# Last layer's edges of a four-layer graph network: messages built in place in PSUM, and the scan of maxima reads them there

## The chip, the cores and the metric

One program on one core of a Trainium2 chip. The metric is the device time of one execution in microseconds (us), the median of the runs shown. The engines are TensorE (PE, its weight loads PEld), VectorE (DVE), ScalarE (ACT), GpSimd (POOL) and SyncE (SP).

## The reference, cut to what matters

Four graph layers run over 3125 nodes of 128 features and 100000 edges, sorted by their target node; each layer is followed by a residual and a layer norm. Only the edges of the last layer are touched. The target's part of a message doesn't vary within a segment, so the kernel adds it after the maximum; what the edge stage computes is, for each edge, the source's row plus weight times `ww`, and of these the running maximum over each segment of equal targets:

```python
Wd, Ws, ww = (Wm[:H], Wm[H:2 * H], Wm[2 * H])
msgs = z[edge_dst] @ Wd + z[edge_src] @ Ws + edge_weight[:, None] * ww[None, :] + bm
agg = jax.ops.segment_max(msgs, edge_dst, num_segments=n)
```

## The kernel before

The edges are laid on 128 partitions (lanes) of T = 784 edges each (the last lane is padded). `layer3_edges` goes through them in TURNS = 28 turns of BODY = 28 edges for each lane, a turn in two halves of HALF = 14. `m.table3` in HBM holds the product of each node's row with `Ws` (the source part); `m.rows3` in HBM takes the running maxima, one row for each edge, and `layer3_nodes` later picks the last row of every segment.

What each engine does in a turn, in the order of its own queue, is written out by hand; only semaphores tie the queues together:

- POOL (lines 2350 to 2362) gathers the source rows: one indirect DMA for each edge position, 128 rows of 512 bytes, into `feat[h]`. Half 0 takes 14 of them, half 1 takes HALF - FOUND = 10 (in turn 0 both take 14). Before a half's gathers it waits for the indices (`staged`) and for `summed`, which says that the half's earlier content of `feat[h]` has been added.
- PE (2436 to 2446) finds the other FOUND = 4 rows of half 1: 75 matmuls of three bf16 parts of the table with one-hot matrices `hot[b]` (25 blocks) into bank 0 of PSUM (`found`), and after ScalarE has copied that out (2423), 4 transposes into bank 2 (`rows_found`). The one-hots of a turn are made by VectorE in the turn before: the first 13 around the scan of half 0, the other 12 around the scan of half 1 (one ahead of the scan, the rest behind it). PE's loop (2438) asks for them 7 blocks ahead.
- ACT: `scale` (2382) writes for each edge position `edge_w` times that edge's weight, 14 or 10 activations of 128 elements, into `scaled_w`, which lies in banks 4 to 7 of PSUM, edge by edge, features contiguous. `turn_back` (2401) reorders the maxima of the half before into `rows[h]` for the store; `spread_resets` (2395) writes the resets of a coming half; `next_indices` (2377) stages the indices of the next turn's gathers. Their order in the loop is: scale of half 0, turn_back of half 1 of the turn before, spread_resets of half 1, the copy of `found`, next_indices of half 0, scale of half 1, turn_back of half 0, spread_resets of the next half 0, next_indices of half 1.
- DVE, `half` (2474): a copy (2477) carries the last maxima of the half before into column 0 of `msg`; the add (2481) writes `feat + scaled_w` into `msg`, which is laid out feature by feature with 15 positions each (so the add's output steps 15 elements); in half 1 four operations (2487) make the messages of the found rows; then the scan (2497) goes over all 128 x 15 = 1920 positions: `state = max(state + resets, msg)`, written to `maxima[h]`. `resets[h]`, `msg` and `maxima[h]` all lie in SBUF (the arena).
- SP loads the keys of the one-hots (2324) and stores `rows[h]` (2328), 896 KB for each half.

There is one `msg` and one `scaled_w`; `feat`, `maxima`, `resets` and `rows` have two buffers each.

Of the kernel before, what the change touches and what calls it, by code (L numbers as in the profile page):

```python
# [9 lines left out]
ALU = mybir.AluOpType  # L10
ACT = mybir.ActivationFunctionType
# [3 lines left out]
N, D, E = 3125, 128, 100000  # L15
# [3 lines left out]
HALF = 14  # L19
# [24 lines left out]
FOUND = 4  # L44
# [12 lines left out]
BIG = 1e30  # L57
# [2221 lines left out]
def layer3_edges(nc, m, I):  # L2279

    with phase(nc, "layer3_edges") as sem:
        A = Arena(m)
        feat = [A(HALF, D) for _ in range(2)]
        msg = A(D, HALF + 1)
        maxima = [A(D, HALF + 1) for _ in range(2)]
        rows = [A(HALF, D) for _ in range(2)]
        tab = A(NB, D)
# [5 lines left out]
        act_vals = A(BODY)  # L2293
        idx = [A(HALF, dt=I32) for _ in range(2)]
        block_ids = A(NB)
        ps = m.psum
        found = ps[:, 0, :]
        rows_found = ps[:, 2, :].rearrange("p (k f) -> p k f", f=D)
        scaled_w = ps[:, 4:8, :].rearrange("p a (k f) -> p (a k) f", f=D)[:, 0:HALF, :]

        begun = sem("states_begun")
        ids_made = sem("block_ids_made")
# [6 lines left out]
        summed, found_summed, carried, scanned = sem("messages_summed"), sem("found_messages_summed"), sem("maxima_carried"), sem("halves_scanned")  # L2309
# [6 lines left out]
        with nc.Block() as block:  # L2316
# [47 lines left out]
            @block.scalar  # L2364
            def _(eng):
                for h in range(2):
                    eng.activation(idx[h], m.src[:, h * HALF:(h + 1) * HALF], ACT.Copy).then_inc(staged[h], 1)

                def split():
                    for k, (a, b) in enumerate(TAB_HALF):  # L2370
                        eng.wait_ge(tab_in[k], 16)
                        eng.activation(parts[0][:, a:b, :], tab[:, a:b, :], ACT.Copy).then_inc(high_made, 1)
                    for k, (a, b) in enumerate(TAB_HALF):
                        eng.wait_ge(rest_made, k + 1)
                        eng.activation(parts[1][:, a:b, :], tab[:, a:b, :], ACT.Copy).then_inc(mid_made, 1)

                def next_indices(i, h, before):

                    hold(eng, landed[h], 16 * before)
                    eng.activation(idx[h], m.src[:, bass.ds(i * BODY + BODY + h * HALF, HALF)], ACT.Copy).then_inc(staged[h], 1)  # L2380

                def scale(i, h, n):

                    eng.wait_ge(summed, 2 * i + h + 1)
                    if h == 0:
                        if not isinstance(i, int):
                            eng.wait_ge(found_summed, i * FOUND - FOUND + 1)
                        eng.activation(act_vals, m.val[:, bass.ds(i * BODY, BODY)], ACT.Copy).then_inc(vals_staged, 1)
                        eng.wait_ge(vals_staged, i + 1)
                    for j in range(n):  # L2390
                        s = h * HALF + j
                        t = eng.activation(scaled_w[:, j, :], m.edge_w[:, :], ACT.Copy, scale=act_vals[:, s:s + 1])
                    t.then_inc(scaled, 1)

                def spread_resets(i, h):

                    hold(eng, scanned, 2 * i + h)
                    eng.activation(resets[h][:, :, 1:HALF + 1],
                                   spread(m.reset[:, bass.ds(i * BODY + h * HALF, HALF)], 1, [P, D, HALF]), ACT.Copy).then_inc(spread_out[h], 1)

                def turn_back(i, h):

                    eng.wait_ge(scanned, 2 * i + h + 2)
                    eng.wait_ge(stored[h], 16 * i + 16)
                    eng.activation(rows[h], maxima[h][:, :, 1:HALF + 1].rearrange("p f t -> p t f"), ACT.Copy).then_inc(turned_back[h], 1)

                eng.wait_ge(begun, 2)
                spread_resets(0, 0)
                spread_resets(0, 1)
                scale(0, 0, HALF)  # L2410
                split()
                next_indices(0, 0, HALF)
                scale(0, 1, HALF)
                turn_back(0, 0)
                spread_resets(1, 0)
                next_indices(0, 1, HALF)
                with eng.Fori(1, TURNS) as i:
                    scale(i, 0, HALF)
                    turn_back(i - 1, 1)
                    spread_resets(i, 1)  # L2420
                    eng.wait_ge(hot_used, i * NB + NB)
                    eng.wait_ge(turned, i)
                    eng.activation(turned_rows, found, ACT.Copy).then_inc(evicted, 1)
                    next_indices(i, 0, i * HALF + HALF)
                    scale(i, 1, HALF - FOUND)
                    turn_back(i, 0)
                    spread_resets(i + 1, 0)
                    next_indices(i, 1, i * (HALF - FOUND) + HALF)
                turn_back(TURNS - 1, 1)
# [19 lines left out]
            def _(eng):  # L2449
# [24 lines left out]
                def half(i, h, n, before, hots):  # L2474

                    eng.wait_ge(scanned, 2 * i + h + 1)
                    eng.tensor_copy(msg[:, :, 0], maxima[1 - h][:, :, HALF]).then_inc(carried, 1)
                    eng.wait_ge(landed[h], 16 * before)
                    eng.wait_ge(scaled, 2 * i + h + 1)
                    by_edge = msg.rearrange("p f t -> p t f")  # L2480
                    eng.tensor_tensor(by_edge[:, 1:n + 1, :], feat[h][:, 0:n, :], scaled_w[:, 0:n, :], ALU.add).then_inc(summed, 1)  # L2481
                    if n < HALF:
                        eng.wait_ge(turned, i + 1)
                        eng.wait_ge(vals_staged, i + 1)
                        for j in range(n, HALF):
                            s = h * HALF + j
                            eng.scalar_tensor_tensor(out=by_edge[:, j + 1, :], in0=m.edge_w[:, :], scalar=act_vals[:, s:s + 1],  # L2487
                                                     in1=rows_found[:, j - n, :], op0=ALU.mult, op1=ALU.add).then_inc(found_summed, 1)
                    for hot_of in hots[:1]:
                        one_hot(*hot_of)  # L2490
                    eng.wait_ge(spread_out[h], i + 1)
                    eng.wait_ge(carried, 2 * i + h + 1)
                    eng.wait_ge(summed, 2 * i + h + 2)
                    if n < HALF:
                        eng.wait_ge(found_summed, i * FOUND + 1)
                    eng.wait_ge(turned_back[h], i)
                    eng.tensor_tensor_scan(maxima[h].rearrange("p f t -> p (f t)"), resets[h].rearrange("p f t -> p (f t)"),  # L2497
                                           msg.rearrange("p f t -> p (f t)"), -BIG, ALU.add, ALU.max).then_inc(scanned, 1)
                    for hot_of in hots[1:]:
                        one_hot(*hot_of)  # L2500

# [225 lines left out]
```

## Time and profile before

| | us |
|---|---|
| median of 3 runs | 5445.45 (5445.11 to 5450.29) |
| profiled execution, its own time | 5450.11 |
| span of the profiled execution | 5448.4 |
| PE, DVE, ACT, POOL busy | 1991.3 (37%), 3728.0 (68%), 2105.0 (39%), 3924.3 (72%) |
| last layer's edges: first gather to last scan's end | 4329.3 to 5369.7 |

The page of the profile sums over eleven stages that run one behind the other with a barrier between them, so busy shares of the whole span say little about this one. The stage of the change is 1040 us long, from 4329 to 5370 us of the span, and its turns repeat closely; one turn from the middle, from 4800 to 4836 us, is shown for each engine. In a timeline row stand the start, the duration, the engine, the line, the operation with output<-input, how many alike are merged, and in brackets how long the engine sat idle before it and what ended that.

### The profile page before, as it was taken

To read this page: it belongs to the slowest core of one execution; us is meant where nothing else is said; L and a number is where in the kernel's file an instruction comes from. 1 tells how busy PE (TensorE), PEld (TensorE's weight loads), DVE (VectorE), ACT (ScalarE), POOL (GpSimd) and SP (SyncE) were. 2 spreads that over 40 slices of the span, in tenths; PEclk is the share of its full clock that TensorE was granted. 3 is DMA by queue.
4 is the path that set the end of the run, shared out by engine and by line. 5 is a ranking of instruction groups with operands and counts; after the bars stand their busy time and mean duration, and the time that the engine had idled before them with its cause. 6 is when DMAs were issued, how large, how long until landed. Compare 5 with 4: busy or idle time off the path is not lost. (4 is left out here: it accounts for less than half of the span.)

```text
span 5448.4 us, 55911 instructions
## 1 busy us (share of the span) xinstructions
PE 1991.3 (37%) x9749; PEld 999.4 (18%) x9749; DVE 3728.0 (68%) x7733; ACT 2105.0 (39%) x5941; POOL 3924.3 (72%) x2991
## 2 busy tenths in 40 slices
PE   2699999999500000000011000000000556665664
PEld 1354444444300000000011000000000322222222
DVE  9676666665578888888876666666666665656665
ACT  0333333332328778778731000000000354454442
POOL 0688888887168777777725888888886188878774
PEclk9899999999755555555555555555555777777777
DMA  9555555555336666666643555555554123232232
GB/s 403 158 103 102 97 98 95 99 102 108 85 102 243 222 236 227 246 236 230 223 169 131 173 174 176 171 168 171 176 175 139 36 93 101 93 102 92 94 102 67
DMA packets 283514, 819.47 MB, mean 150 GB/s; under 512 B 63269, under 2 KB 178485, under 8 KB 271250
## 3 DMA queue, kind: packets, MB, share of 16 engines
q1 hardware_dynamic: 99250, 504.98, 25.1%
q0 software_dynamic: 171504, 252.10, 21.3%
q10 hardware_dynamic: 12528, 60.37, 2.7%
q14 instruction: 219, 1.79, 0.1%
q8 instruction: 13, 0.21, 0.0%
HBM read 368.73 MB, written 448.51 MB: 150 GB/s over the span
## 5 line engine op out<-in xcount | busy, mean ns | idle before, releaser
L1864 POOL DMA_INDIRECT arena<-table,arena x784 | 989.5, 1262 | 238.9 <-issue 238.9
L624 POOL DMA_INDIRECT tab<-arena x560 | 986.9, 1762 | 189.7 <-issue 147.3
L2353 POOL DMA_INDIRECT arena<-table,arena x676 | 824.1, 1219 | 206.6 <-issue 205.5
L746 PE MATMUL psum<-arena 128*128 128x512 bf16 (+1 forms) x4704 | 958.9, 359 | 0.0
L1514 PE MATMUL psum<-ident,arena 128*128 128x128 f32 x15 | 3.7, 428 | 2533.9 <-DVEq L1542 2533.9
L1287 POOL DMA_INDIRECT arena<-table,arena x588 | 719.8, 1224 | 189.4 <-issue 178.1
L2440 PE MATMUL psum<-arena 128*128 128x512 bf16 x2025 | 580.1, 455 | 290.6 <-DVE arena L2472 171.0
L1333 ACT ACTIVATE arena<-arena 128x128 f32<-128x128 f32 x1974 | 598.7, 387 | 186.1 <-DVE arena L1441 123.6
L1441 DVE SCALAR_TENSOR_TENSOR arena<-arena 128x512 f32<-128x512 f32 x728 | 544.9, 749 | 13.4 <-issue 1.2
L746 PEld LDWEIGHTS psum<-arena 128*128 128x128 bf16 x4704 | 436.4, 99 | 480.6 <-issue 36.7
L1514 PEld LDWEIGHTS psum<-ident,arena 128*128 128x128 f32 x15 | 2.7, 213 | 2534.6 <-DVEq L1542 2534.4
L2481 DVE TENSOR_TENSOR arena<-arena,psum 128x1792 f32<-128x1792 f32 (+1 forms) x56 | 155.6, 2779 | 402.4 <-DMA arena<-table,arena 326.9
L781 ACT ACTIVATE arena<-psum 128x387 f32<-128x387 f32 x224 | 99.0, 442 | 695.2 <-POOLq L623 509.7
L1935 DVE TENSOR_TENSOR arena<-arena 128x1792 f32<-128x1792 f32 x56 | 113.5, 2027 | 352.5 <-DMA arena<-table,arena 245.4
L2440 PEld LDWEIGHTS psum<-arena 128*128 128x128 bf16 x2025 | 221.7, 113 | 645.1 <-issue 258.7
L682 DVE SCALAR_TENSOR_TENSOR arena<-arena 128x128 f32<-128x128 f32 x784 | 277.0, 353 | 25.4 <-issue 3.2
L1963 DVE SCALAR_TENSOR_TENSOR arena<-arena 128x136 f32<-128x136 f32 x784 | 274.4, 350 | 16.7 <-DVE arena L1956 15.9
L1926 DVE SCALAR_TENSOR_TENSOR arena<-arena 128x128 f32<-128x128 f32 x784 | 269.9, 344 | 15.9 <-issue 8.8
L649 DVE SCALAR_TENSOR_TENSOR arena<-arena 128x3 f32<-128x3 f32 x224 | 49.6, 221 | 322.1 <-ACT arena L781 321.9
L1287 POOL DMA_INDIRECT xT<-table,arena x196 | 223.2, 1139 | 59.8 <-issue 58.8
L671 DVE TENSOR_SCALAR arena<-arena 128x3125 bf16<-128x3125 f16 x224 | 237.8, 1062 | 0.9 <-PE psum L746 0.9
L2497 DVE TENSOR_TENSOR_SCAN arena<-arena 128x1920 f32<-128x1920 f32 x56 | 232.3, 4148 | 0.4 <-DVE arena L2487 0.2
(408 smaller groups left out, 4595.2 us busy)
## 6 DMA issues: line engine op xcount, KB each, us to landing
rows<-arena SPq DMA_DIRECT2D x56, 3808.0 KB
arena<-seg_rows SPq DMA_DIRECT2D x112, 896.0 KB
rows<-arena SPq DMA_DIRECT2D x56, 1008.0 KB
seg_rows<-arena ACTq DMA_DIRECT2D x28, 1792.0 KB
rows<-arena SPq DMA_DIRECT2D x56, 896.0 KB
arena<-table,arena POOLq DMA_INDIRECT x2048
arena<-src_lanes SPq DMA_DIRECT2D x56, 448.0 KB
tab<-arena POOLq DMA_INDIRECT x560
```

What stands on the lines that cost most here:

```text
L624: eng.indirect_dma_start(out=m.tabs[j], out_offset=bass.IndirectOffsetOnAxis(ap=idx[g][:, k:k + 1], axis=0), in_=rows[g][:, k, 0:D], in_of ...
L671: eng.tensor_scalar(hot[n % HOTS], m.node_ids, of[:, CENTRED, s:s + 1], None, ALU.is_equal).then_inc(hot_made, 1)
L682: eng.scalar_tensor_tensor(out=xr[h][:, j, :], in0=prev, scalar=keeps[:, s:s + 1], in1=xr[h][:, j, :], op0=ALU.mult, op1=ALU.add).then_inc ...
L746: t = eng.matmul(ps[:, c, 0:w], part[n // 2 % PAIRS][:, n % 2, :], hot[n % HOTS][:, lo:lo + w], start=False, stop=False, skip_group_check= ...
L1287: eng.indirect_dma_start(out=feat[k][:, j, :], out_offset=None, in_=m.table1, in_offset=bass.IndirectOffsetOnAxis(ap=idx[k][:, j:j + 1], a ...
L1333: eng.activation(apart[:, t, r * D:(r + 1) * D], feat[k][:, t, 0:D], ACT.Copy, scale=hot[k % 2][:, t, r:r + 1]).then_inc(masked, 1)
L1441: v.put(eng.scalar_tensor_tensor(out=row[:, j, 0:SUM], in0=row[:, j - 1, 0:SUM] if j else old, scalar=keeps[h][:, j:j + 1], in1=apart[:, j ...
L1864: eng.indirect_dma_start(out=kv[k][:, j, :], out_offset=None, in_=m.table2, in_offset=bass.IndirectOffsetOnAxis(ap=idx[k][:, j:j + 1], axi ...
L1926: eng.scalar_tensor_tensor(out=q[k][:, j, :], in0=q[k][:, j - 1, :] if j else q[k - 1][:, HALF - 1, :], scalar=carry_keeps[k % 2][:, j:j + ...
L1963: v.put(eng.scalar_tensor_tensor(out=row[:, j, 0:MAX], in0=row[:, j - 1, 0:MAX] if j else old, scalar=keeps[h][:, j:j + 1], in1=row[:, j, ...
L2353: eng.indirect_dma_start(out=feat[h][:, j, :], out_offset=None, in_=m.table3, in_offset=bass.IndirectOffsetOnAxis(ap=idx[h][:, j:j + 1], a ...
L2440: t = eng.matmul(found, part[:, b, :], hot[b], start=(b == 0 and p == 0), stop=(b == NB - 1 and p == 2))
```

## The change

`msg` moves from SBUF to banks 4 to 7 of PSUM, over the place of `scaled_w`, which is gone. ScalarE writes the scaled weights straight into the places of the messages (steps of 15 elements), VectorE adds the gathered rows to them in place, and the scan reads its second input from PSUM; `resets` and `maxima` stay in SBUF. Since the one buffer is now written by `scale`, `scale` of a half waits until the scan of the half before has read it (`scanned` in place of `summed`), and the wait for `found_summed` ahead of it goes. The carry copy moves from ahead of the add, before the wait for the gathered rows, to behind it.

```diff
-        msg = A(D, HALF + 1)
...
-        scaled_w = ps[:, 4:8, :].rearrange("p a (k f) -> p (a k) f", f=D)[:, 0:HALF, :]
+        msg = ps[:, 4:8, :].rearrange("p a c -> p (a c)")[:, 0:D * (HALF + 1)]
+        by_edge = msg.rearrange("p (f t) -> p t f", t=HALF + 1)
...
                 def scale(i, h, n):
 
-                    eng.wait_ge(summed, 2 * i + h + 1)
+                    eng.wait_ge(scanned, 2 * i + h + 1)
                     if h == 0:
-                        if not isinstance(i, int):
-                            eng.wait_ge(found_summed, i * FOUND - FOUND + 1)
                         eng.activation(act_vals, m.val[:, bass.ds(i * BODY, BODY)], ACT.Copy).then_inc(vals_staged, 1)
                         eng.wait_ge(vals_staged, i + 1)
                     for j in range(n):
                         s = h * HALF + j
-                        t = eng.activation(scaled_w[:, j, :], m.edge_w[:, :], ACT.Copy, scale=act_vals[:, s:s + 1])
+                        t = eng.activation(by_edge[:, j + 1, :], m.edge_w[:, :], ACT.Copy, scale=act_vals[:, s:s + 1])
                     t.then_inc(scaled, 1)
...
                     eng.wait_ge(scanned, 2 * i + h + 1)
-                    eng.tensor_copy(msg[:, :, 0], maxima[1 - h][:, :, HALF]).then_inc(carried, 1)
                     eng.wait_ge(landed[h], 16 * before)
                     eng.wait_ge(scaled, 2 * i + h + 1)
-                    by_edge = msg.rearrange("p f t -> p t f")
-                    eng.tensor_tensor(by_edge[:, 1:n + 1, :], feat[h][:, 0:n, :], scaled_w[:, 0:n, :], ALU.add).then_inc(summed, 1)
+                    eng.tensor_tensor(by_edge[:, 1:n + 1, :], feat[h][:, 0:n, :], by_edge[:, 1:n + 1, :], ALU.add).then_inc(summed, 1)
+                    eng.tensor_copy(by_edge[:, 0, :], maxima[1 - h][:, :, HALF]).then_inc(carried, 1)
...
                     eng.tensor_tensor_scan(maxima[h].rearrange("p f t -> p (f t)"), resets[h].rearrange("p f t -> p (f t)"),
-                                           msg.rearrange("p f t -> p (f t)"), -BIG, ALU.add, ALU.max).then_inc(scanned, 1)
+                                           msg, -BIG, ALU.add, ALU.max).then_inc(scanned, 1)
```

## Rows read from the trace of the kernel before

**Rows 1.** Waits of VectorE and GpSimd, 4400 to 5360 us: who, for whom, total, times, longest.

```profile
DVE arena L2481 <- DMA arena<-table,arena: 289.5, 40, 8.9
...
POOL arena L2353 <- issue: 191.8, 629, 0.3
POOL arena L2353 <- DVE arena L2481: 0.3, 1, 0.3
```

**Rows 2.** Gathers grouped: whole run, then the first 18, then one turn, 4800 to 4836.44.

```profile
L2353 POOL DMA_INDIRECT arena<-table,arena x676 | 824.1, 1219 | 206.6 <-issue 205.5 <-ACT arena L2367 0.8 <-DVE arena L2481 0.3
...
L2353 POOL DMA_INDIRECT arena<-table,arena x18 | 17.1, 947 | 6.0 <-issue 5.2 <-ACT arena L2367 0.8
...
L2353 POOL DMA_INDIRECT arena<-table,arena x25 | 33.8, 1351 | 7.6 <-issue 7.3 <-DVE arena L2481 0.3
```

**Rows 3.** Timeline of GpSimd, one turn from held gather to held gather.

```profile
4798.74 4.63 POOL L2353 DMA_INDIRECT arena<-table,arena  x1 [0.30 <-issue]
...
4816.17 0.94 POOL L2353 DMA_INDIRECT arena<-table,arena  x1 [0.30 <-issue]
4817.42 3.70 POOL L2353 DMA_INDIRECT arena<-table,arena  x1 [0.31 <-issue]
...
4832.67 0.95 POOL L2353 DMA_INDIRECT arena<-table,arena  x1 [0.31 <-issue]
...
4835.18 4.64 POOL L2353 DMA_INDIRECT arena<-table,arena  x1 [0.30 <-DVE arena L2481]
```

**Rows 4.** Timeline of VectorE in that turn.

```profile
4798.47 4.14 DVE L2497 TENSOR_TENSOR_SCAN arena<-arena 128x1920 f32<-128x1920 f32 x1
...
4812.77 2.32 DVE L2481 TENSOR_TENSOR arena<-arena,psum 128x1280 f32<-128x1280 f32 x1 [6.28 <-DMA arena<-table,arena]
4814.93 1.18 DVE L2487 SCALAR_TENSOR_TENSOR arena<-edge_w,arena,psum 128x128 f32<-128x128 f32 x4
4815.96 0.34 DVE L2472 TENSOR_SCALAR arena<-arena 128x512 bf16<-128x512 f16 x1
4816.21 4.16 DVE L2497 TENSOR_TENSOR_SCAN arena<-arena 128x1920 f32<-128x1920 f32 x1
4820.28 3.45 DVE L2472 TENSOR_SCALAR arena<-arena 128x512 bf16<-128x512 f16 x11
4823.66 0.26 DVE L2477 COPY arena<-arena 128x128 f32<-128x128 f32 x1
4831.61 3.21 DVE L2481 TENSOR_TENSOR arena<-arena,psum 128x1792 f32<-128x1792 f32 x1 [7.69 <-DMA arena<-table,arena]
...
4834.91 4.16 DVE L2497 TENSOR_TENSOR_SCAN arena<-arena 128x1920 f32<-128x1920 f32 x1
```

**Rows 5.** Timeline of VectorE and GpSimd behind the stage: a scan with a PSUM input.

```profile
5378.19 0.42 DVE L2633 TENSOR_TENSOR_SCAN arena<-whole_neg,psum 128x128 f32<-128x128 f32 x1 [0.39 <-PE psum L2596]
5378.34 0.95 POOL L2548 DMA_INDIRECT arena<-rows,first_end  x1 [19.12 <-POOLq L103]
```

**Rows 6.** Timeline of ScalarE in that turn.

```profile
4816.50 4.16 ACT L2392 ACTIVATE psum<-edge_w,arena 128x128 f32<-128x128 f32 x14
4820.60 3.28 ACT L2405 ACTIVATE arena<-arena 128x1792 f32<-128x1792 f32 x1
4823.78 1.69 ACT L2398 ACTIVATE arena<-reset 128x1792 f32 x1
4837.81 0.60 ACT L2423 ACTIVATE arena<-psum 128x512 f32<-128x512 f32 x1 [12.34 <-DMA arena<-table]
4838.41 2.98 ACT L2392 ACTIVATE psum<-edge_w,arena 128x128 f32<-128x128 f32 x10
```

**Rows 7.** Timeline of TensorE, then its busy time and granted clock, 4820.6 to 4835.

```profile
4820.66 13.25 PE L2440 MATMUL psum<-arena 128*128 128x512 bf16 x51 [2.85 <-DVE arena L2472]
...
4820.60:4835.00 14.40, 13.25 (x51) 5.41 (x51) 0.85 0.38 123
```

**Rows 8.** An add in layer 2 with contiguous operands, grouped, 2946 to 4157 us.

```profile
L1935 DVE TENSOR_TENSOR arena<-arena 128x1792 f32<-128x1792 f32 x56 | 113.5, 2027 | 352.5 <-DMA arena<-table,arena 245.4 <-issue 107.1
```

## The prediction

> **What bounds the kernel now.** I read the waits of the stage first, because eleven stages run one behind the other and the page's busy shares mix them. VectorE waits 289.5 us for gathered rows ahead of its add, while GpSimd, which issues the gathers, waits for an engine once, for 0.3 us; all its other idle time is "issue", 0.3 us ahead of each gather [rows 1]. So the gathers set the length of the turns, and VectorE, ScalarE and TensorE follow.
>
> Then I asked what a gather costs. The first 18 of the stage, before any scan, take 947 ns each; over all 676 the mean is 1219, in the sample turn 1351 [rows 2]. The timelines say which are long: the gather issued at 4798.74 takes 4.63 us, the one at 4817.42 takes 3.70, the one at 4835.18 takes 4.64 [rows 3]. Put beside VectorE [rows 4]: scans run from 4798.47 to 4802.61, from 4816.21 to 4820.37 and from 4834.91 to 4839.07, and the three long gathers end 0.76, 0.75 and 0.75 us behind those ends. The gather at 4816.17, issued 0.04 us ahead of a scan, takes 0.94. A gather issued while the scan runs is held until it ends. Gathers issued within the add (4832.67, inside 4831.61 to 4834.82) take 0.95. The add has one input in SBUF and one in PSUM; the scan has both in SBUF.
>
> A turn is 4835.18 - 4798.74 = 36.44 us: 24 gathers at 1.25 us (0.947 and 0.30 of issue), 30.0, and two holds, 3.68 and 2.75 us, together 6.4.
>
> **The holds.** The change leaves the scan one SBUF input, the resets. What the trace shows of such operations is that gathers pass beside them at full speed: the add above, and, nearer, the only scan of the run with a PSUM input, 5378.19 to 5378.61: a gather issued at 5378.34 within it takes 0.95 us, where a hold until 0.75 us behind its end would have made it 1.02 [rows 5]. I take the holds as gone; the other end is that none goes. Their sum: 676 x (1.219 - 0.947) = 184 us [rows 2]; about 2 us of it I leave standing, by estimate, for the two subtractions of `split`, which keep two SBUF inputs. Gain 182 us. By the sample turn it is 27 x 6.4 + 3.7 = 177.
>
> The Trainium skill (SBUF — State Buffer, Who interferes with whom) says that a VectorE instruction with two SBUF inputs takes the read interface it shares with GpSimd and shuts out a GpSimd instruction that reads SBUF. By that rule the holds go, and the rows agree for the scans. The same place infers that `tensor_tensor` leaves descriptor generation alone, since that would need the write interface; taken so, the scan wouldn't hold either, and the gain would be nil; the 4.63 us gathers speak against it.
>
> **The scan itself.** 1920 elements take 4.16 us from SBUF, the 128 of the PSUM scan 0.42 [rows 4, 5]: a slope of (4.16 - 0.42) / 1792 = 2.09 ns an element, and 1920 x 2.09 = 4.01 leaves 0.15 fixed, 0.27 + 0.15 = 0.42 for 128. Both lie on one line, so reading PSUM costs the scan nothing.
>
> **Steps of 15 elements in PSUM.** No row shows them; bounds from both sides. ScalarE's scale is 4.16 us for 14, 0.297 each [rows 6]. It moves from contiguous to stepped writes. Lower bound: no change. Upper: what a stepped access costs ScalarE in SBUF, 3.28 us for 1792 elements against 1.69 [rows 6], 0.89 ns an element, 0.11 us an operation: +1.6 us for 14, +1.1 for 10. The add (3.21 and 2.32 us [rows 4]) writes in steps already, into SBUF; with contiguous operands 1792 elements take 2.03 [rows 8]. Lower bound: PSUM takes steps at no cost, 2.03, so -1.2 us. Upper: its read is stepped now as well and costs as much as ScalarE's, +1.6 and +1.1. I take both as unchanged, since the add's own row with a stepped write is nearest; the upper end decides a rival. The Trainium skill (Advanced Engine Details and Errata, PSUM Cachelines) has lines of 8 bytes there and asks for pairs of consecutive elements; steps of 60 bytes never give one. By that the upper end would be the likelier.
>
> **The waits.** One buffer now serves `scale`, add and scan, so two loops get tighter, and 30.0 us is the turn they must fit in.
> Loop A, scan to scale to add to scan, over both halves: scale 4.16 + 0.23 for staging the weights + 2.98, adds 3.21 + 2.32, found rows 1.18, copies 2 x 0.26, one-hots ahead of the scans 2 x 0.34, scans 2 x 4.16 [rows 4, 6], with six handovers of 0.1: 24.2 us. It has 5.8 us to spare; at the upper bounds (+5.4) it is 29.6.
> Loop B goes through TensorE: one-hots are made behind the scan of half 1, 51 matmuls follow, `found` is copied out, and only then does ScalarE's queue reach the scale of half 1. From the scan's end at 4820.37 to the copy at 4837.81 is 17.4 us, the copy and the scale of 10 are 3.6 [rows 6], and from the add of half 1 to the scan's end VectorE takes 7.6, plus the copy that is now there, 0.26 [rows 4]: 28.9 us. Before, this scale was followed by 7.8 us of waiting for rows (4841.4 to 4849.2), so it cost nothing. Now 1.1 us are left. With the upper bounds, +2.2, it is 31.1.
>
> What else is queued: behind the longer wait of `scale` on ScalarE stand turn_back, which waits for the same scan anyway, spread_resets and next_indices. For half 0 they are due only when the copy of `found` comes, 12 us later [rows 6]. The indices of the next half 0 stand behind the copy of `found`, 0.2 us later; by loop B's times they come some 2 us before GpSimd is through with the ten gathers of half 1. SP's stores depend on turn_back and stay two buffers ahead. The carry copy was hidden in the wait for rows and comes to stand on VectorE's path, 0.26 us a half; while the gathers bound the turn it costs only at the last half, 0.3 us. The wait for `found_summed` was past whenever the scan is. The new end of each path is the landing of the gathers again, in turns of 30.0 us.
>
> **Sum.** Profiled execution 5450.1 - 182 + 0.3 = 5268. The median of the runs is 4.7 us under it: 5264.
>
> **Rivals.**
> 1. A loop takes over. Stepped PSUM accesses cost the upper bounds, or TensorE's clock is low in the 51 matmuls (it is 0.85 of full speed there, between its two levels, and 13.25 us busy [rows 7]; at 1.2 GHz, half, they would be 22.5). For: loop B has 1.1 us of room. Against: TensorE stood idle for 2.85 us ahead of this stretch [rows 7], and shorter turns leave less idle time. Upper bounds: (31.1 - 30.0) x 27 = 30 us back, 5294; twice these: 33.3, 5353; the low clock alone, (28.9 + 22.5 - 13.25 - 30.0) = 8.2 at worst, 5485 at the far end; as the clock was low for part already, I price it at half, 4.6 us a turn, which gives 33.5 and 5359.
> 2. The hold belongs to the scan as such, not to its second SBUF input. The turn stays 36.4 us; time 5445. For: every hold of the stage proper is a scan's. Against: the scan of [rows 5], a margin of 0.07 us.
> 3. Slower: stepped writes and in-place adds in PSUM are several times dearer. It decides once loop B grows by 7.5 us, past 36.4. With 5 ns an element: ten scales 10 x (0.64 + 0.19 - 0.30) = +5.3, the add 1280 x 5 ns + 0.1 - 2.32 = +4.2, the found rows 4 x 0.5 = +2: 40.4 us a turn, 27 x 4.0 more than now, 5553. Nothing in the trace is that dear (the worst step here is 1.8 ns an element).
>
> **How the numbers follow.** Forecast 0.70 (5264), rival 1 0.19, rival 2 0.07, rival 3 0.04. Range: the forecast with some 10 us for the holds' sum, and rival 1 up to a turn of 32.6 us (2.6 x 27 = 70), 5255 to 5335. A measurement can tell 0.2% (11 us) from no change. Faster: forecast and nearly all of rival 1, 0.89; same: rival 2, 0.07; slower: rival 3, 0.04.
>
> **What would show it.** Right: gathers of 947 ns mean throughout with none over 1.1 us beside a scan, a turn of 30.0 us, and VectorE still waiting for rows ahead of its add. Rival 1: GpSimd waits for ScalarE's indices or VectorE's add, the add waits for `scale`. Rival 2: gathers of 4.6 us remain. The operations at 2392 and 2481 show the price of the steps at once. The prediction fails most easily in loop B, by 1.1 us of room in a turn.

## The result

The changed kernel took 5274.39 us (median of 4 runs, 5271.81 to 5275.44) against 5447.78 us before, measured beside it: ratio 0.9681, 95% interval 0.9664 to 0.9698, 173 us faster. 5264 was forecast, in a range of 5255 to 5335. Run again later on two other chips (below), the same file gave this time on one and 5520 us, slower than before, on the other, so part of this document is about why the forecast held and part about why it doesn't hold everywhere.

The profiled execution took 5273.86 us, with a span of 5272.1. First the grouped lines of the changed kernel over the stage: busy time, mean ns of one, then idle time ahead.

```profile
L2353 POOL DMA_INDIRECT arena<-table,arena x676 | 671.9, 994 | 208.2 <-issue 203.4 <-DVE psum L2477 3.4 <-ACT arena L2367 0.8
...
L2494 DVE TENSOR_TENSOR_SCAN arena<-arena,psum 128x1920 f32<-128x1920 f32 x56 | 232.4, 4150 | 0.5 <-DVE psum L2484 0.2
...
L2390 ACT ACTIVATE psum<-edge_w,arena 128x128 f32<-128x128 f32 x676 | 201.5, 352 | 143.6 <-DVE arena L2494 142.7
...
L2477 DVE TENSOR_TENSOR psum<-arena,psum 128x1792 f32<-128x1792 f32 x29 | 58.8, 2029 | 268.5 <-DMA arena<-table,arena 268.5
L2477 DVE TENSOR_TENSOR psum<-arena,psum 128x1280 f32<-128x1280 f32 x27 | 40.4, 1497 | 42.6 <-DMA arena<-table,arena 42.6
L2484 DVE SCALAR_TENSOR_TENSOR psum<-edge_w,arena,psum 128x128 f32<-128x128 f32 x108 | 30.3, 349 | 0.0
```

The gathers answer [rows 2]: 824.1 us have become 671.9, the mean 1219 ns has become 994. The scan is as long as it was [rows 4]. The in-place add takes 2029 ns where it took 3.21 us [rows 4], as much as the contiguous add of [rows 8]. The scale keeps its length. Then the timeline of one turn, VectorE's rows first, GpSimd's behind them.

```profile
4936.64 4.15 DVE L2494 TENSOR_TENSOR_SCAN arena<-arena,psum 128x1920 f32<-128x1920 f32 x1
4940.71 3.83 DVE L2470 TENSOR_SCALAR arena<-arena 128x512 bf16<-128x512 f16 x12
4946.05 1.50 DVE L2477 TENSOR_TENSOR psum<-arena,psum 128x1280 f32<-128x1280 f32 x1 [1.52 <-DMA arena<-table,arena]
...
4949.04 4.15 DVE L2494 TENSOR_TENSOR_SCAN arena<-arena,psum 128x1920 f32<-128x1920 f32 x1
4953.10 2.96 DVE L2470 TENSOR_SCALAR arena<-arena 128x512 bf16<-128x512 f16 x11
4965.74 2.03 DVE L2477 TENSOR_TENSOR psum<-arena,psum 128x1792 f32<-128x1792 f32 x1 [9.68 <-DMA arena<-table,arena]
...
4940.98 0.94 POOL L2353 DMA_INDIRECT arena<-table,arena  x1 [0.30 <-issue]
...
4950.97 0.94 POOL L2353 DMA_INDIRECT arena<-table,arena  x1 [0.30 <-issue]
4952.22 0.94 POOL L2353 DMA_INDIRECT arena<-table,arena  x1 [0.30 <-issue]
4953.47 2.71 POOL L2353 DMA_INDIRECT arena<-table,arena  x1 [0.31 <-issue]
4956.48 0.94 POOL L2353 DMA_INDIRECT arena<-table,arena  x1 [0.30 <-issue]
```

Gathers now pass within the scan of 4949.04 to 4953.19 at 0.94 us, and none of the 165 that the stage issues within a scan takes more than 0.95; the holds of [rows 3] are gone. But one gather is still long, and it is a new kind: issued at 4953.47, 0.37 us into the row of 11 one-hots that follows the scan of half 1, it ends at 4956.18, 0.12 behind the end of that row (4956.06). The row of 12 at 4940.71 holds nobody; its operations are 0.32 us apart (3.83 / 12) where those of the closed row are 0.27 apart (2.96 / 11). 17 of the 27 turns have such a gather, 2.62 to 2.79 us long, and take about 31.8 us; most of the others take 30.0. That is some 17 x 1.75 = 30 us that the prediction has no word for.

Last, the waits over 4400 to 5200 us (who, for whom, total, times, longest), beside [rows 1].

```profile
DVE psum L2477 <- DMA arena<-table,arena: 285.1, 52, 9.8
...
ACT psum L2390 <- DVE arena L2494: 136.3, 26, 6.4
...
ACT arena L2421 <- PE psum L2438: 97.0, 26, 4.9
...
POOL arena L2353 <- DVE psum L2477: 2.4, 8, 0.3
```

VectorE still waits for rows and GpSimd for almost nobody: the gathers still set the turn. ScalarE, which before sat idle for under 1 us in all directly ahead of its scales, now waits 136.3 us there for the scan of half 0, and it costs nothing: the add behind it still waits for rows.

Where the 176.25 us between the two profiled executions (5450.11 and 5273.86) lie, by the first and last gather of the stage: the gather stretch went from 1029.9 to 879.3 us (150.6), it begins 16.2 us earlier (4313.1, not 4329.3), and what lies behind its end shrank from 89.2 to 79.7 us (9.5). But for 1.6 us between the last gather and the last scan, the last two terms are in code that the change doesn't touch.

### The profile page after: what moved, and what is told of

It is laid out like the page before. It is cut to its first block and busy times, and to the rows that moved or that the text cites. A ratio compares the mean times of both kernels' runs of the same rounds, so it can differ in the third digit from the quotient of the medians.

```text
span 5272.1 us, 55718 instructions
## 1 busy us (share of the span) xinstructions
PE 1925.0 (37%) x9583; PEld 990.1 (19%) x9749; DVE 3665.7 (70%) x7733; ACT 2103.1 (40%) x5941; POOL 3773.8 (72%) x2991
## 3 DMA queue, kind: packets, MB, share of 16 engines
q1 hardware_dynamic: 99250, 504.98, 26.3%
## 5 line engine op out<-in xcount | busy, mean ns | idle before, releaser
L1864 POOL DMA_INDIRECT arena<-table,arena x784 | 995.6, 1270 | 238.8 <-issue 238.8
L746 PE MATMUL psum<-arena 128*128 128x512 bf16 (+1 forms) x4592 | 930.1, 358 | 6.3 <-issue 0.4
L1287 POOL DMA_INDIRECT arena<-table,arena x588 | 710.7, 1209 | 183.9 <-issue 178.3
L2353 POOL DMA_INDIRECT arena<-table,arena x676 | 671.9, 994 | 208.2 <-issue 203.4
L2438 PE MATMUL psum<-arena 128*128 128x512 bf16 x1971 | 530.6, 434 | 306.1 <-DVE arena L2470 263.3
L2477 DVE TENSOR_TENSOR psum<-arena,psum 128x1792 f32<-128x1792 f32 (+1 forms) x56 | 99.3, 1772 | 311.1 <-DMA arena<-table,arena 311.1
L2390 ACT ACTIVATE psum<-edge_w,arena 128x128 f32<-128x128 f32 x676 | 201.5, 352 | 143.6 <-DVE arena L2494 142.7
L1884 ACT ACTIVATE arena<-src 128x14 int32 x56 | 12.0, 214 | 566.4 <-DMA arena<-table,arena 566.2
```

Of the source, the lines that this page charges most:

```text
L746: t = eng.matmul(ps[:, c, 0:w], part[n // 2 % PAIRS][:, n % 2, :], hot[n % HOTS][:, lo:lo + w], start=False, stop=False, skip_group_check= ...
L1287: eng.indirect_dma_start(out=feat[k][:, j, :], out_offset=None, in_=m.table1, in_offset=bass.IndirectOffsetOnAxis(ap=idx[k][:, j:j + 1], a ...
L1864: eng.indirect_dma_start(out=kv[k][:, j, :], out_offset=None, in_=m.table2, in_offset=bass.IndirectOffsetOnAxis(ap=idx[k][:, j:j + 1], axi ...
L2353: eng.indirect_dma_start(out=feat[h][:, j, :], out_offset=None, in_=m.table3, in_offset=bass.IndirectOffsetOnAxis(ap=idx[h][:, j:j + 1], a ...
L2390: t = eng.activation(by_edge[:, j + 1, :], m.edge_w[:, :], ACT.Copy, scale=act_vals[:, s:s + 1])
L2438: t = eng.matmul(found, part[:, b, :], hot[b], start=(b == 0 and p == 0), stop=(b == NB - 1 and p == 2))
```

## The experiments

Twelve runs in four jobs, each job on one chip with the kernel before timed beside it. The table shows all of them, by what their profiles say of the stage: the stretch from first to last gather, the mean gather, and how long behind the end of the scan of half 1 the copy of `found` starts (us, range over the turns without the first of them).

| kernel | chip | us | ratio to before, interval | stretch | gather ns | copy of `found` |
|---|---|---|---|---|---|---|
| before | - | 5445.45 | | 1029.9 | 1219 | 17.3-18.9 |
| after | - | 5274.39 | 0.9681 [0.9664, 0.9698] | 879.3 | 994 | 11.5-14.2 |
| e4 before again | 14 | 5443.99 | one run | 1029.3 | 1218 | 17.5-19.0 |
| e1 waits alone | 14 | 5445.28 | 0.9997 [0.9987, 1.0006] | 1031.6 | 1222 | 19.1-24.1 |
| e2 weights in SBUF | 14 | 5441.40 | 0.9998 [0.9989, 1.0008] | 1026.1 | 1030 | 25.0-26.0 |
| e3 row broken | 14 | 5519.56 | 1.0130 [1.0109, 1.0151] | 1094.5 | 951 | 26.4-30.6 |
| e5 turn back first | 10 | 5237.26 | 0.9625 [0.9609, 0.9641] | 846.6 | 948 | 12.9-14.5 |
| e6 after again | 10 | 5270.04 | 0.9684 [0.9668, 0.9700] | 871.7 | 983 | 11.5-14.3 |
| e7 = e2 | 4 | 5446.56 | 0.9990 [0.9978, 1.0001] | 1023.1 | 1029 | 25.1-25.9 |
| e8 = e3 | 4 | 5521.10 | 1.0131 [1.0102, 1.0161] | 1091.0 | 948 | 26.3-30.1 |
| e9 = after | 4 | 5520.03 | 1.0129 [1.0100, 1.0159] | 1090.6 | 951 | 26.9-30.1 |
| e10 = e5 | 9 | 5246.96 | 0.9634 [0.9606, 0.9662] | 846.5 | 948 | 12.8-14.5 |
| e11 copy of `found` last | 9 | 5252.93 | 0.9645 [0.9617, 0.9673] | 852.5 | 953 | 21.5-22.2 |
| e12 two parts | 9 | 5249.87 | 0.9639 [0.9609, 0.9670] | 860.0 | 966 | 9.3-10.7 |

The kernel before took 5443.54, 5440.37, 5449.13 and 5447.22 us (medians) on chips 14, 10, 4 and 9.

### The first job: what holds a gather

**e1**, the kernel before with the waits and the order of the changed one, the messages still in SBUF:

```diff
-                    eng.wait_ge(summed, 2 * i + h + 1)
+                    eng.wait_ge(scanned, 2 * i + h + 1)
                     if h == 0:
-                        if not isinstance(i, int):
-                            eng.wait_ge(found_summed, i * FOUND - FOUND + 1)
...
-                    eng.tensor_copy(msg[:, :, 0], maxima[1 - h][:, :, HALF]).then_inc(carried, 1)
...
+                    eng.tensor_copy(msg[:, :, 0], maxima[1 - h][:, :, HALF]).then_inc(carried, 1)
```

> The kernel before with only the new waits and order: scale waits for the scan of the half before, the carry copy stands behind the add; messages stay in SBUF. My theory: a gather issued while the scan reads two SBUF inputs is held, and nothing else of the change matters; the scans still hold gathers, so 5448 us within 0.2%, mean gather about 1219 ns. Rival, the new waits by themselves shift the turn enough to change the time: a turn more than 0.5 us off 36.4, over 13 us in all.

Measured: no difference, and gathers of 1222 ns as before. The waits by themselves give and cost nothing while the scans hold the gathers, though the copy of `found` comes later (19.1 to 24.1 us, where e4 has 17.5 to 19.0); the gain is in where the messages lie.

**e2**, the changed kernel with the scaled weights in SBUF, so that the add reads two SBUF operands and the scan one:

```diff
+        scaled_w = A(HALF, D)
...
-                        t = eng.activation(by_edge[:, j + 1, :], m.edge_w[:, :], ACT.Copy, scale=act_vals[:, s:s + 1])
+                        t = eng.activation(scaled_w[:, j, :], m.edge_w[:, :], ACT.Copy, scale=act_vals[:, s:s + 1])
...
-                    eng.tensor_tensor(by_edge[:, 1:n + 1, :], feat[h][:, 0:n, :], by_edge[:, 1:n + 1, :], ALU.add).then_inc(summed, 1)
+                    eng.tensor_tensor(by_edge[:, 1:n + 1, :], feat[h][:, 0:n, :], scaled_w[:, 0:n, :], ALU.add).then_inc(summed, 1)
```

> The changed kernel, but ScalarE writes the scaled weights contiguously to SBUF, so that the add has two SBUF inputs and one output in PSUM; the scan still reads PSUM. Theory (two SBUF inputs of VectorE hold the gathers): the scans hold none, the adds hold one gather each, for 0.2 to 1.8 us, about 1.9 us a turn, so some 50 us above the changed kernel's 5274: 5325. Rival (the hold belongs to the scan as an operation, and a plain add takes no part): 5274, no long gather beside an add.

The timeline of e2, one turn, VectorE and then GpSimd:

```profile
4716.98 2.03 DVE L2478 TENSOR_TENSOR psum<-arena 128x1792 f32<-128x1792 f32 x1 [8.66 <-DMA arena<-table,arena]
...
4719.56 4.15 DVE L2495 TENSOR_TENSOR_SCAN arena<-arena,psum 128x1920 f32<-128x1920 f32 x1
...
4734.60 1.50 DVE L2478 TENSOR_TENSOR psum<-arena 128x1280 f32<-128x1280 f32 x1 [7.18 <-ACT arena L2391]
...
4717.98 1.84 POOL L2354 DMA_INDIRECT arena<-table,arena  x1 [0.30 <-issue]
...
4720.13 0.94 POOL L2354 DMA_INDIRECT arena<-table,arena  x1 [0.30 <-issue]
...
4732.33 0.94 POOL L2354 DMA_INDIRECT arena<-table,arena  x1 [5.03 <-ACT arena L2381]
...
4734.83 2.08 POOL L2354 DMA_INDIRECT arena<-table,arena  x1 [0.30 <-issue]
```

The holds have moved from the scan to the add. A gather issued within the add of 4716.98 to 4719.01 takes 1.84 us and ends 0.81 behind it; the next, within the scan, takes 0.94. So a hold goes with VectorE reading two operands from SBUF, in the add as in the scan, and rival 2 (the scan as such) falls. The Trainium skill says the same of the read interface (SBUF — State Buffer, Who interferes with whom), and infers there that descriptor generation is left alone; these rows speak against the inference.

The trace of before could have settled rival 2 without a run. The subtractions of `split` read two SBUF operands and are no scans; VectorE's rows of them, and the gathers beside them:

```profile
4359.29 3.60 DVE L2463 TENSOR_TENSOR arena<-arena 128x1536 f32<-128x1536 f32 x2
4362.81 3.62 DVE L2466 TENSOR_TENSOR arena<-arena 128x1536 bf16<-128x1536 f32 x2
...
4360.55 1.36 POOL L2353 DMA_INDIRECT arena<-table,arena  x1 [0.31 <-issue]
4362.21 1.49 POOL L2353 DMA_INDIRECT arena<-table,arena  x1 [0.30 <-issue]
4364.01 1.37 POOL L2353 DMA_INDIRECT arena<-table,arena  x1 [0.30 <-issue]
4365.68 1.57 POOL L2353 DMA_INDIRECT arena<-table,arena  x1 [0.30 <-issue]
```

Each of the four holds one gather, until 0.82 us behind its own end. The size of e2's holds was as expected too: 676 x (1.030 - 0.947) = 56 us.

The time was not. 5325 was expected, 5441 came: GpSimd waits 5.03 us for ScalarE's indices (L2381), which stand behind the copy of `found`, and that comes 25 to 26 us behind the scan. Loop B of the prediction (through TensorE) had taken over.

**e3**, the changed kernel with a nop after every third one-hot, to open the closed row:

```diff
-                    for hot_of in hots[1:]:
+                    for k, hot_of in enumerate(hots[1:]):
                         one_hot(*hot_of)
+                        if k % 3 == 2:
+                            eng.engine_nop()
```

> The changed kernel with an empty operation on VectorE after every third one-hot behind the scan. In the changed kernel 17 gathers of 2.6 to 2.8 us end 0.1 us behind a row of eleven one-hots. Theory: back-to-back one-hots keep GpSimd out, and a gap lets the gather in; then nearly all of these are at most 1.1 us, 17 x 1.75 = 30 us less, 5245. Rival (the gap is too short, or the row holds as a whole, whatever stands in it): the long gathers stay, 5274 or a little more.

There was no held gather beyond the four of `split` and three of 1.1 us (mean 951), yet the time is 5519.56, 275 us above the 5245 expected. Read alone this says that breaking the row frees the gathers and that seven nops a turn cost 250 us; e8 and e9 show that neither follows.

**e4** is the kernel before, unedited, for its profile on that chip.

> The kernel before, unchanged, for a second profile. Between the first two profiles stages that the change doesn't touch differ by 16 us ahead of the last layer's edges and by 8 us behind them. If that comes with the program, this profile has the stage lengths of the first (layer 1 edges 1257 us, the last layer's nodes 71 us) within 2 us; if it is spread between executions, it does not.

It repeats the profile of before to 0.6 us in the stretch of gathers. Of the two stages that its expectation names, the last layer's nodes repeat (70.9 us against 70.7) and layer 1's edges don't (1252 against 1257): that much lies between two executions of one kernel.

### The second job: the held gather in the row of one-hots

**e5** has ScalarE turn the maxima back ahead of the scale of half 1, which moves the row of one-hots against the gathers:

```diff
                     next_indices(i, 0, i * HALF + HALF)
-                    scale(i, 1, HALF - FOUND)
                     turn_back(i, 0)
+                    scale(i, 1, HALF - FOUND)
```

> The changed kernel with ScalarE's turn_back of half 0 ahead of the scale of half 1, instead of behind it: no more work, 3.3 us more between that scan and the scaled weights. Loop B then is longer by 3.3 us. If gathers bound the turn with the room that the changed kernel's profile shows (copy of found 13.2 us behind the scan, loop B 24.7), nothing changes: 5274. If TensorE is as late as in the kernel before (17.4, loop B 28.9), the turn is 32.2 us and the time some 57 us over the changed kernel's.

**e6** is the changed kernel, unedited, on the same chip.

> The changed kernel, unchanged, a second time. In the profiles of the kernels with the waits alone, with the weights in SBUF and with the broken row, TensorE's marks come late: the copy of found starts 17 to 30 us behind the scan of half 1, against 11.5 to 14 in the changed kernel's first profile, and these profiles hold a third as many records of semaphore updates. If TensorE's lateness belongs to those programs, this run repeats the first: 5274 us, copy of found 11.5 to 14 us behind the scan, turns of 30.0 or 31.8. If it belongs to the chip or the recording, TensorE is late here too and loop B sets the turn: 33 to 37 us, 5350 to 5450.

e6 repeats the result. e5 is 33 us faster by the medians. Its grouped gathers and its row of one-hots:

```profile
L2353 POOL DMA_INDIRECT arena<-table,arena x676 | 640.9, 948 | 206.5 <-issue 196.6
...
4953.51 4.14 DVE L2494 TENSOR_TENSOR_SCAN arena<-arena,psum 128x1920 f32<-128x1920 f32 x1
4957.57 3.46 DVE L2470 TENSOR_SCALAR arena<-arena 128x512 bf16<-128x512 f16 x11
```

The row is 0.31 us an operation (3.46 / 11) and holds nobody; every turn takes 29.95 to 30.07 us. The stretch is 846.6 against 871.7: 25.1 us for the 13 held gathers of e6, 13 x 1.75 = 23, and two turns with an extra idle stretch of about 1 us. The other 8 us of the medians lie outside the stretch or between executions.

The edit shifted the phase, and the kept traces say which phase holds. All 37 gathers held by a row (17 in the changed kernel, 13 in e6, 1 in e11, 6 in e12) were issued 0.28 to 0.45 us behind the start of a row of 11. Between 0.34 and 0.45 us others pass, at 0.94 to 1.08; every one issued later passes. In e5 and e10 none falls into that stretch. Beside the rows of 12 none is held, though in the changed kernel and in e6 many are issued there too. Why the one row holds and the other doesn't is open. The Trainium skill (SBUF — State Buffer, Who interferes with whom) has `tensor_scalar` among the operations that can take both shared interfaces, for the whole instruction and for whoever issues first. One instruction is 0.27 us here, so a gather shut out for a row of 11 goes beyond what that says, and the rows beside which gathers pass show that it isn't the rule for every such row.

### The third job: the same program, 250 us apart

e1 to e4 had run on one chip and e5 and e6 on another, and in the first group TensorE was late throughout. So e2, e3 and the changed kernel went to one chip together.

> The kernel with the weights in SBUF (e2) once more, now on one chip with the kernel of the change and with the broken row. It took 5441 us and its copy of `found` came 25 to 26 us behind the scan of half 1, against 11.5 to 14 in the kernel of the change, but the two had been run in different jobs. If TensorE's lateness belongs to the program: 5441 again, stage 1049, copy of `found` 25 us behind the scan. If it belongs to the chip or the job: the copy comes some 12 to 14 us behind the scan in all three kernels of this job (or 20 or more in all three), and this one takes 5274 + 55 - 30 = about 5300, the holds beside the adds alone.

> The kernel with a nop after every third one-hot (e3) once more, on one chip with the kernel of the change. Program: 5520 again, GpSimd waiting some 250 us for ScalarE's indices, copy of `found` 27 to 30 us behind the scan. Chip or job: 5237 to 5245, no held gathers, the copy 12 to 14 us behind the scan.

> The kernel of the change, unedited, on the chip of the two before. Program: 5270 to 5274, stage 890 to 897, copy of `found` 11.5 to 14.5 us behind the scan of half 1, some 14 to 18 held gathers. Chip or job: a copy that comes over 20 us behind the scan, and a time over 5400.

e9 is the changed kernel, unedited, and takes 5520.03 us, 1.3% over the kernel before on the same chip (5449.13). The lateness goes with the chip or the job, not with the program; each job ran on a chip of its own, so the two can't be told apart. I call jobs in which TensorE is late as here late jobs, and those like the second, in which it isn't, prompt jobs. e3's nops are cleared of the cost: e8 and e9 agree within 1.1 us. They are not shown to free a gather either: e9, without them, holds none beside a row, and in e3, e8 and e9 none is issued less than 0.6 us behind the start of a row of 11. What the nops do in a prompt job isn't known.

What lateness looks like, in weight loads of TensorE: start, duration, count, idle time ahead. First e9.

```profile
4856.73 4.20 PEld L2438 LDWEIGHTS psum<-arena 128*128 128x128 bf16 x20 [0.23 <-issue]
4862.27 0.10 PEld L2438 LDWEIGHTS psum<-arena 128*128 128x128 bf16 x1 [1.35 <-issue]
4864.47 0.10 PEld L2438 LDWEIGHTS psum<-arena 128*128 128x128 bf16 x1 [2.11 <-issue]
4867.37 0.11 PEld L2438 LDWEIGHTS psum<-arena 128*128 128x128 bf16 x1 [2.80 <-issue]
4869.54 0.11 PEld L2438 LDWEIGHTS psum<-arena 128*128 128x128 bf16 x1 [2.06 <-issue]
4872.36 0.10 PEld L2438 LDWEIGHTS psum<-arena 128*128 128x128 bf16 x1 [2.72 <-issue]
4875.15 0.10 PEld L2438 LDWEIGHTS psum<-arena 128*128 128x128 bf16 x1 [2.69 <-issue]
4877.28 0.14 PEld L2438 LDWEIGHTS psum<-arena 128*128 128x128 bf16 x2 [2.02 <-issue]
```

Then e6, the same program on chip 10.

```profile
4883.30 8.08 PEld L2438 LDWEIGHTS psum<-arena 128*128 128x128 bf16 x38 [0.16 <-issue]
4892.63 0.42 PEld L2443 LDWEIGHTS psum<-ident,arena 128*128 128x128 f32 x4 [1.25 <-issue]
```

In e6 38 loads follow one another at 0.21 us. In e9 about six a turn come 2.1 to 2.9 us apart with no engine and no transfer named as what they wait for, some 15 us, and then the pace is back. Their one-hots had been ready since 4855.83, the end of the row behind the scan of half 1. It isn't the clock. The stretches of e9 (length, busy time and count of matmuls, granted clock, DMA share, GB/s) are before the late loads, in them and behind them:

```profile
4852.80:4861.00 8.20, 8.08 (x29) 0.79 0.25 67
4862.00:4877.00 15.00, 2.95 (x6) 0.66 0.26 82
4877.00:4882.20 5.20, 4.91 (x15) 0.66 0.00 0
```

The granted clock, between its two levels, is the same 0.66 where six matmuls run in 15 us and where 15 run in 5.2. The waits of e9, 4400 to 5200 us:

```profile
PEld psum L2438 <- issue: 472.9, 523, 4.2
ACT arena L2421 <- PE psum L2438: 399.6, 21, 20.8
...
POOL arena L2353 <- ACT arena L2380: 204.3, 21, 14.6
DVE psum L2477 <- ACT psum L2390: 142.0, 21, 9.2
```

The copy of `found` (L2421) waits up to 20.8 us for TensorE; behind it on ScalarE stand the indices, for which GpSimd waits up to 14.6 us, and the scale of half 1, for which the add waits up to 9.2. That is loop B of rival 1, at 39.4 us a turn on average, but without either cost that rival 1 gave for it: the steps in PSUM are cheap here too (the add 2.03 and 1.50 us) and the clock isn't the cause.

The profile of before that the prediction rests on was itself a late one. Its trace and those of e1 to e4 and e7 to e9 hold 42,514 to 47,625 semaphore updates; after, e5, e6 and e10 to e12 hold 72,161 to 72,264, and the two traces of one program, e9 and e6, stand on either side. That before's gather turn of 36.4 us covers the lateness fits its time, which is the same on every chip (5440 to 5449); no profile of it was taken in a prompt job. What lies behind the last gather tells the two apart in one program as well: 97.5 us in e9, 79.1 in e6.

What makes TensorE late is open. None of the edits run in a late job removed it, and none was made to. A trace that keeps fewer semaphore updates could mean that the recording has a part, or only that both have one cause; that TensorE's instructions reach it late is another reading, which no view here can test. The Trainium skill (NOTIFIC — the notification-queue block, Overflow: three behaviours, one of which stalls the engine) says that the block that writes such records has a setting in which a full ring stalls the producer until software drains it. No run here shows whether that is it, nor whether an unrecorded execution would ever be late.

### The fourth job: against the loop through TensorE

e10 is e5 once more. **e11** takes from loop B what needn't be in it:

```diff
                     spread_resets(i, 1)
+                    next_indices(i, 0, i * HALF + HALF)
+                    scale(i, 1, HALF - FOUND)
                     eng.wait_ge(hot_used, i * NB + NB)
                     eng.wait_ge(turned, i)
                     eng.activation(turned_rows, found, ACT.Copy).then_inc(evicted, 1)
-                    next_indices(i, 0, i * HALF + HALF)
-                    scale(i, 1, HALF - FOUND)
                     turn_back(i, 0)
```

**e12** gives TensorE less to do; it leaves out the products of the third part of the table, so its found rows are less exact:

```diff
-                        for p, part in enumerate(parts):
-                            t = eng.matmul(found, part[:, b, :], hot[b], start=(b == 0 and p == 0), stop=(b == NB - 1 and p == 2))
+                        for p, part in enumerate(parts[:2]):
+                            t = eng.matmul(found, part[:, b, :], hot[b], start=(b == 0 and p == 0), stop=(b == NB - 1 and p == 1))
```

> Two conditions have shown for one and the same program: in one (the first runs and those with e5 and e6) the copy of `found` comes 11.5 to 14.5 us behind the scan of half 1 and the kernel of the change takes 5270; in the other (e9) TensorE is late, its weight loads come 2.1 to 2.9 us apart for some 15 us of each turn with nothing waited for, the copy comes 27 to 30 us behind, and it takes 5520. This is the kernel with turn_back ahead of the scale of half 1 (e5) again. In the first condition: 5237, no held gather, turns of 30.0 us. In the second: its order puts 3.3 us of turn_back between the copy of `found` and the scale of half 1, on the loop through TensorE, so up to 27 x 3.3 = 88 us above e9, 5520 to 5610.

> The kernel of the change, with ScalarE's queue in another order: the indices of the next half 0 and the scale of half 1 stand ahead of the copy of `found`, as neither needs it. In the first condition the gathers bound either order: 5237 if no gather meets the row of one-hots, 5274 if as many do as now. In the second condition the loop through TensorE loses the scale (3.0 us) and the add (1.5): from the scan's end 28 to the copy, then 0.6, 0.7, 1.1, 0.4 and 4.2 for copy, transposes, found rows, one-hot and scan, 35 to 36 us a turn where e9 has 39.7: 27 x 4 = about 110 us less than 5520, 5400 to 5420, and under the kernel before. If the order doesn't matter there (TensorE gives out the pace by itself) 5520 stays.

> Leaves out part of the computation: the products of the third bfloat16 part of the table, so TensorE has 34 matmuls a turn, not 51, all else as in the kernel of the change. In the first condition nothing changes beyond the held gathers, 5237 to 5274. In the second: if TensorE lags because of how many instructions it runs, the stretch of loads 2.1 to 2.9 us apart shortens or goes and the time falls by over 27 x 5 = 135 us to between 5240 and 5385; if it lags for a fixed time a turn whatever it runs, only 17 x 0.22 = 3.7 us a turn go, 100 us, 5420.

This job was a prompt one, the first condition of these expectations (72,000 updates, no late loads), so only the first halves of these expectations were tested. e10 repeats e5: ratio 0.9634 against 0.9625, mean gather 948, turns of 29.94 to 30.09. e11 puts the copy of `found` at 21.5 to 22.2 us behind the scan by its place in the queue, and takes 5252.93, which by two runs each can't be told from e10's 5246.96. So in a prompt job some 8 us more in front of the copy cost nothing that shows, in an order in which of VectorE's work only the found rows hang on it. One gather is held in it, 2.72 us. e12 has 34 matmuls where 51 followed the scan of half 1 (50 and 75 over the whole turn, which its expectation left out); it brings the copy 2 to 4 us closer to the scan. The stage's gathers take 860.0 us with six of them held, 13.5 us more than e10's, so fewer matmuls buy nothing here but another phase. Whether e5's or e11's order is better where TensorE is late wasn't run.

## Why the prediction was right, and where it wasn't

- **Gathers bound, holds go.** Right: gathers of 0.94 us beside every scan, turns of 30.0 us where nothing else interferes. The sum wanted a stage 182 us shorter. In e5 and e10, where nothing else holds, the stretch of gathers is 846.6 and 846.5 us, 183.3 and 183.4 under the 1029.9 of before. The changed kernel gives 150.6 of it. The holds left beside `split` are four and cost 2.5 us (1.82, 1.50, 1.37 and 1.57 us, less 4 x 0.947), where 2 were allowed for.
- **A term that was missing.** The one-hots. In the profile of before the row's first gathers were those held by the scan, so none was ever issued in the first 0.8 us behind a scan [rows 3, 4]. Taking the scan's hold away put one there. Asking what a freed gather would meet next would have found the row; its price, 17 x 1.75 = 30 us, stood in no row of before.
- **Why the total was still within 10 us.** The profiled execution should have been 5268 and was 5273.86. The stretch missed by 31 us (150.6, not 182); 25.7 us came from outside it (16.2 ahead, 9.5 behind), which nobody forecast. The part behind goes with the late and prompt jobs: 87.9 to 99.7 us behind the last gather in the late profiles, 77.7 to 81.3 in the prompt ones. The part ahead does so less clearly: the first gather comes at 4323.2 to 4333.1 in the late and at 4306.2 to 4319.6 in the prompt ones, up to 10 and 13 us apart within the two kinds. Neither is a gain of the change. Two errors of some 31 and 26 us cancelled, and that the total came within 10 us is luck.
- **The scan from PSUM** costs the same: 4150 ns against 4148 over the stage. Right.
- **Steps in PSUM.** The scale was taken as unchanged and is (352 ns against 354). The add was taken as unchanged, 3.21 and 2.32 us, and costs 2.03 and 1.50: the lower bound. The found rows fell from 407 to 349 ns; the carry copy, taken as equal, rose from 291 to 373. The nearest row, the add's own, was the wrong guide: its length was that of stepped writes into SBUF. The Trainium skill (Advanced Engine Details and Errata, PSUM Cachelines) wants every two consecutive elements contiguous, by which the upper end would be likelier; neither the scale nor the add bears that out here.
- **Loop A**, 24.2 us in the prediction, never set the turn. **A path that was missed**: the scale of half 1 now waits for the scan of half 0, which ends 6.7 us behind the start of half 0's add (4965.74 to 4968.31 + 4.15 in that turn). In the turn above the scale ends at 4943.83, 2.2 us ahead of the add at 4946.05, so it cost nothing, with 2.2 us of room.
- **Loop B** is the step that failed outside the first measurement. Its 17.4 us came from one profile in which TensorE was late: its last matmul ends at 4833.91 (4820.66 + 13.25, [rows 7]) and the copy starts at 4837.81 [rows 6], 3.9 us later, though by the code it waits for TensorE alone. In the changed kernel's profile that gap is 0.04 us in every turn and the copy comes 11.5 to 14.2 us behind the scan, so the room was 4 to 7 us and not 1.1. In the late e9 the copy came 26.9 to 30.1 us behind. Rival 1 named the loop and the order of events rightly and priced it at 33.5 us a turn; it took 39.4. Its chance of 0.19 was meant for costs of the program; what decided it, in every kernel with messages in PSUM that ran in a late job (e2, e3, e7, e8, e9), was the lateness of TensorE, which the prediction had no word for.
- **Slower** was given 0.04, for dear steps in PSUM. Of the three jobs in which the unedited changed kernel ran, it was slower in one, by 1.3%, and for another reason.

## What to carry to other kernels

When a hold on the bounding engine is taken away, look at what the freed instructions will meet next on the engine that held them, not only at what they met so far; and where a sum leaves 1 us of room on a loop, look in that loop's own rows for time in which nobody is waited for, because such time can grow. Run the unedited kernel again beside every set of experiments, and on more than one chip, before an edit is blamed: the same file was 173 us faster than its forerunner on one chip and 71 us slower on another. And before a run is made, look in the stage's odd corners for the case that parts two rivals: here the four subtractions of `split` were it. Where a loop's length is uncertain, work that doesn't need its result can stand ahead of the wait for it in each queue; that cost nothing measurable in e11, and what it gives where TensorE is late wasn't run.

## What the hardware showed that was not expected

- A scan, an add or a subtraction of VectorE with both operands in SBUF holds a gather issued within it until 0.75 to 0.82 us behind its end (the scan 4.63 us, e2's add 1.84, a subtraction of `split` 1.49); the add and the scan with one operand in PSUM hold none. A gather issued just ahead passes: 0.94 us for one issued 0.04 us before a scan.
- A row of 11 back-to-back `tensor_scalar` operations (bf16 from f16) can shut a gather out until 0.12 us behind the row's last one, or let each gather in for 0.94 to 1.08 us and be 0.03 to 0.05 us slower an operation. Only gathers issued 0.28 to 0.45 us behind the row's start were ever shut out, and not all of those.
- A VectorE add in place in PSUM in steps of 60 bytes runs at the contiguous pace, 2.03 us for 1792 elements a lane, where the same steps written to SBUF cost 3.21 us.
- TensorE can stand for 2.1 to 2.9 us an instruction, some 15 us a turn, with no releaser in the trace, in some jobs (each on a chip of its own) and not in others, with the same program.
